# Row numbers by slot: 32 products of 78 columns in place of 64 products of 39

## Chip, core and metric

One core of a Trainium2 chip runs the whole kernel. The metric is the device time of one execution in microseconds (us), from three executions: 375.12, 373.69 and 374.58, median 374.58.

## What is computed

Two layers. The first is a mixture of experts over 2048 tokens of 256 channels: layer norm, a norm over time, a style from a small network, then a router that picks 2 of 8 experts for each token, and the experts (256 to 1024 to 256) on the picked tokens. The second is a finite-difference stencil on the result.

```python
h = h_norm * gamma[:, None, :] + beta[:, None, :]
h_flat = h.reshape(-1, D)
probs = jax.nn.softmax(h_flat @ router_w, axis=-1)
gates, idx = jax.lax.top_k(probs, TOPK)
gates = gates / gates.sum(-1, keepdims=True)
combine = jnp.zeros((N, E), h_flat.dtype).at[jnp.arange(N)[:, None], idx].add(gates)
hid = jax.nn.relu(jnp.einsum('nd,edf->nef', h_flat, exp_w1) + exp_b1)
eout = jnp.einsum('nef,efd->ned', hid, exp_w2) + exp_b2
y = jnp.einsum('ned,ne->nd', eout, combine)
return x + y.reshape(x.shape)
...
df = -gradv_Af + gradvv_Bf * 0.5
f_new = f + df * dt[:, None, None]
return jnp.maximum(f_new, 0.0)
```

## The kernel before

The kernel computes each expert only for the tokens that picked it. The 4096 pairs of token and choice are sorted by expert into columns of 128 rows. There are NC = 39 columns, served in NS = 23 slots; a slot is two columns wide, every third slot is one column wide (`width`).

The prologue norms and transposes the tokens, writes them as rows to DRAM (`h_rows`), and gets the router's logits on the way. VectorE then picks the two experts of each token (lines 1073 to 1091), TensorE counts ranks with products of ones (lines 838 to 844), and VectorE works out the place of each pair: `slot_i`, split into a column number (`col_f`) and a row in the column (`low_f`).

The step that matters here turns places around: for each place it needs the number of the pair that goes there. The pairs lie in TC = TOPK * NJ = 32 tiles of 128. For each tile t, `oh_row[:, :, t]` is a one-hot matrix of pair against row, and `oh_col[:, :, t]` one of pair against column. The number of a pair is 1 + partition + 128 t, in two parts so that each is exact in bf16: `tok[:, 0, :, :]` is `oh_col` times (partition + 1), written by ScalarE (line 551), `tok[:, 1, :, :]` is `oh_col` times 128 t, written by VectorE (line 1154). TensorE multiplies `oh_row` of tile t with each part of `tok` of tile t and sums all 64 products in one psum row of 39 columns (lines 849 to 855). `oh_row` comes in four chunks of eight tiles (lines 1156 to 1161), and TensorE waits for each chunk (`ohrow_ok`). The layout has the tile as the innermost index of `tok`, `oh_row` and `oh_col`.

Behind the last product (`perm_mm`) VectorE reads the psum row: `num_i` is the number as an integer, `src_cur` the source rows of the first two slots, `src_i` those of all, `dst_i` the destinations, with a large number where a place is empty (lines 1162 to 1173). In VectorE's code `link` makes the next instruction wait for this one by a semaphore, and `chained` only counts it, so that the next `link` waits for both.

GpSimd's queue waits for `src_cur` (`src_ok`) and gathers the rows of slots 0 and 1 by indirect DMA (line 735). When the first gather has landed (`rows_in[0]`), three engines go on: TensorE transposes the rows (line 866), VectorE makes the low part of the first expert matrix (line 1184), and SyncE issues the loads of the second expert matrices of slots 0 and 1 (lines 427 to 431). ScalarE and VectorE split every expert matrix into a high and a low part (`w_split`), as they do with the rows and the hidden layer, and TensorE multiplies three pairs of parts. Its order is written out by hand: `turn(0)`, `layer1(0)` with `turn(1)` in its middle, then for each slot k `layer1(k + 1)`, `turn(k + 2)`, `layer2(k)`. ScalarE's order for slot 0 is the split of the second matrix (`split_w2`) ahead of the hidden layer. Results go to DRAM (`y_rows`) by indirect DMA, and the stencil is worked out after the last slot.

Of the kernel before, what the change touches and what calls it, by code (L numbers as in the profile page):

```python
# [7 lines left out]
ALU = mybir.AluOpType  # L8
ACT = mybir.ActivationFunctionType
F32 = mybir.dt.float32  # L10
F32R = mybir.dt.float32r
BF16 = mybir.dt.bfloat16
# [3 lines left out]
P = 128  # L16
NB, T, D = 8, 256, 256
N = NB * T
NJ = N // P
KD = D // P  # L20
E, FF, TOPK = 8, 1024, 2
# [5 lines left out]
NC = ROWS + E - 1  # L27
# [3 lines left out]
EMPTY = 8192.0  # L31
# [89 lines left out]
def moe_then_stencil(nc, x, ids, dt, exp_w1, exp_b1, exp_w2, exp_b2, a_grid, b_grid, small, consts, out):  # L121
# [4 lines left out]
    with ctx:  # L126
        def sb(name, shape, dt_=F32):
            return ctx.enter_context(nc.sbuf_tensor(name, shape, dt_))
# [5 lines left out]
        banks = [psum[:, i, :] for i in range(8)]  # L134
# [7 lines left out]
        dst_i = sb("dst_i", [P, NC], I32)  # L142
# [13 lines left out]
        with ExitStack() as phase:  # L156
            def own(name, shape, dt_=F32):
                return phase.enter_context(nc.sbuf_tensor(name, shape, dt_))
# [15 lines left out]
        with ExitStack() as phase:  # L174
            def own(name, shape, dt_=F32):
                return phase.enter_context(nc.sbuf_tensor(name, shape, dt_))

            h_pre = own("h_pre", [P, KD, N])
            hT = own("hT", [P, KD, N])
            own("w_split_first", [P, 10240])  # L180

            z = own("z", [P, 4, D])
            tok = own("tok", [P, 2, NC, TOPK * NJ], BF16)
            own("w_split_last", [P, 6144 - 1024 - TOPK * NJ * NC])
            h_tok = own("h_tok", [P, NJ, KD, P + E])
            oh_row = own("oh_row", [P, P, TOPK * NJ], BF16)
            oh_col = own("oh_col", [P, NC, TOPK * NJ], BF16)
            eye_rw = own("eye_rw", [P, KD, P + E])
            before_bf = own("before_bf", [P, P], BF16)
            ones_bf = own("ones_bf", [P, P], BF16)  # L190
            st1 = own("st1", [P, NJ, 6])
            mv1 = own("mv1", [P, NJ, 2])
            var1 = own("var1", [P, NJ])
            rs1 = own("rs1", [P, NJ])
            st2 = own("st2", [P, NB, KD, 6])
            mv2 = own("mv2", [P, NB, KD, 2])
            var2 = own("var2", [P, NB, KD])
            rs2 = own("rs2", [P, NB, KD])
            half = own("half", [P, 8])
            warm = own("warm", [P, 8])  # L200
            aff_a = own("aff_a", [P, NB, KD])
            aff_m = own("aff_m", [P, NB, KD])
            aff_b = own("aff_b", [P, NB, KD])

            id_i = own("id_i", [S_SUB, NB], I32)
            id_f = own("id_f", [S_SUB, NB])
            oh_s = own("oh_s", [S_SUB, NB])
            small_sb = own("small_sb", [P, SMALL_ALL])
            se_t = own("se_t", [SE, NB])
            hy1 = own("hy1", [SH, NB])  # L210
            hy2 = own("hy2", [SH, NB])
            sy1 = own("sy1", [SH // 2, NB])
            sty = own("sty", [P, 4, NB])
            gabs = own("gabs", [P, KD, NB])
            grelu = own("grelu", [P, KD, NB])
            gexp = own("gexp", [P, KD, NB])
            gln = own("gln", [P, KD, NB])
            gsum = own("gsum", [P, KD, NB])
            gam = own("gam", [P, KD, NB])

            lg = own("lg", [P, NJ, E])
            eq = own("eq", [P, NJ, E])
            cand = own("cand", [P, NJ, E])
            least = own("least", [P, NJ])
            oh = own("oh", [P, TOPK, NJ, E])
            lg2 = own("lg2", [P, NJ, E])
            gap = own("gap", [P, NJ])
            e2 = own("e2", [P, NJ])
            den = own("den", [P, NJ])
            m_bf = own("m_bf", [P, NJ, E], BF16)  # L230
            cnt_i = own("cnt_i", [P, E], I32)
            tl_i = own("tl_i", [P, 2, E], I32)
            tl_f = own("tl_f", [P, 2, E])
            t_end = own("t_end", [P, 2, E])
            t_off = own("t_off", [P, 2, E])
            base = own("base", [P, E])
            room = own("room", [P, E])
            jump = own("jump", [P, E])
            late = own("late", [P, NJ, E])
            pos = own("pos", [P, NJ, E])  # L240
            pick = own("pick", [P, TOPK, NJ, E])
            slot_f = own("slot_f", [P, TOPK * NJ])
            slot_i = own("slot_i", [P, TOPK * NJ], I32)
            low_i = own("low_i", [P, TOPK * NJ], I32)
            col_i = own("col_i", [P, TOPK * NJ], I32)
            low_f = own("low_f", [P, TOPK * NJ], BF16)
            col_f = own("col_f", [P, TOPK * NJ], BF16)
            row_of = own("row_of", [P, P, TOPK * NJ], BF16)
            col_of = own("col_of", [P, NC, TOPK * NJ], BF16)
            tile_of = own("tile_of", [P, TOPK * NJ], BF16)  # L250
            e_cmp = own("e_cmp", [1, 2, NS, E])
            e_sum = own("e_sum", [1, NS])
            num_i = own("num_i", [P, NC], I32)
            num_f = own("num_f", [P, NC])

        def part(name):
            rows, cols, at = SMALL[name]
            return small_sb[0:rows, at:at + cols]
# [88 lines left out]
        def field(g):  # L347
            return FV[0] if g == 0 else x_sb[:, 4 * g:4 * g + 4, :].rearrange("p j d -> p (j d)")
# [124 lines left out]
        def _(act):  # L473
# [52 lines left out]
            for i in range(NB + 4):  # L526
# [16 lines left out]
                if 0 <= i - 4 < LATE:  # L543
# [4 lines left out]
            act.activation(e2[:, :], gap[:, :], ACT.Exp).then_inc(e2_ok, 1)  # L548

            act.wait_ge(ohcol_ok, 1)  # L550
            act.activation(tok[:, 0, :, :], oh_col[:, :, :], ACT.Copy,
                           scale=cst[:, C_PART + 1:C_PART + 2]).then_inc(tok0_ok, 1)

            def split_w1(k, m, first=False):
# [117 lines left out]
            for g in range(NPAIR):  # L672
# [3 lines left out]
                for i in range(2):  # L676
# [4 lines left out]
                    else:  # L681
                        act.wait_ge(y2_added[g], 16)
                    last = act.activation(FD[g % 2][:, 512 * i:512 * i + 512], field(g)[:, 512 * i:512 * i + 512],
                                          ACT.Copy, scale=dt_b[:, 2 * g + i:2 * g + i + 1])
# [92 lines left out]
        def _(pe):  # L777
# [64 lines left out]
            for j in range(NJ):  # L842
                last = pe.matmul(banks[3][:, 0:E], ones_bf[:, :], m_bf[:, j, :], start=(j == 0), stop=(j == NJ - 1))
# [5 lines left out]
            for t in range(TOPK * NJ):  # L849
                if t % CHUNK == 0:  # L850
                    pe.wait_ge(ohrow_ok, t // CHUNK + 1)
                for part in range(2):
                    last = pe.matmul(banks[1][:, 128:128 + NC], oh_row[:, :, t], tok[:, part, :, t],  # L853
                                     start=(t == 0 and part == 0), stop=(t == TOPK * NJ - 1 and part == 1))
            last.then_inc(perm_mm, 1)

            def turn(k, m):
# [96 lines left out]
            for g in range(NPAIR + 1):  # L954
                if g >= 1:
                    pe.wait_ge(t_s, g)
                    for q in range(2):
                        last = rows_mm(g - 1, q, ident, SM[(g - 1) % 2], q, stop=True)
# [13 lines left out]
        def _(dve):  # L972
            steps = [0]

            def link(ins):

                steps[0] += 1
                ins.then_inc(chain, 1)
                dve.wait_ge(chain, steps[0])

            def chained(ins):

                steps[0] += 1
                ins.then_inc(chain, 1)
# [94 lines left out]
            for c, src in enumerate((lg, lg2)):  # L1079
# [4 lines left out]
                                              op0=ALU.mult, op1=ALU.add))  # L1084
                link(dve.tensor_reduce(least[:, :], cand[:, :, :], AX_X, ALU.min))
                link(dve.tensor_tensor(oh[:, c, :, :], cand[:, :, :], spread(least[:, :]), ALU.is_equal))
                if c == 0:
                    link(dve.scalar_tensor_tensor(out=lg2[:, :, :], in0=oh[:, 0, :, :], scalar=-3e38,
                                                  in1=lg[:, :, :], op0=ALU.mult, op1=ALU.add))
# [32 lines left out]
            def by_token(v):  # L1122
# [6 lines left out]
                                             op0=ALU.mult, op1=ALU.add))  # L1129
# [17 lines left out]
            def by_tile(v, n):  # L1147
                return v.rearrange("p (a t) -> p a t", a=1).broadcast_to([P, n, TC])
# [2 lines left out]
            dve.tensor_tensor(oh_col[:, :, :], by_tile(col_f[:, :], NC), col_of[:, :, :],  # L1151
                              ALU.is_equal).then_inc(ohcol_ok, 1)
            dve.wait_ge(ohcol_ok, 1)
            dve.tensor_tensor(tok[:, 1, :, :], oh_col[:, :, :], by_tile(tile_of[:, :], NC),
                              ALU.mult).then_inc(tok_ok, 1)
            for n in range(TC // CHUNK):
                at = slice(CHUNK * n, CHUNK * n + CHUNK)
# [2 lines left out]
                    low_f[:, at].rearrange("p (a t) -> p a t", a=1).broadcast_to([P, P, CHUNK]), row_of[:, :, at],  # L1160
                    ALU.is_equal).then_inc(ohrow_ok, 1)
            dve.wait_ge(perm_mm, 1)
            num = banks[1][:, 128:128 + NC]

            link(dve.tensor_scalar(num_i[:, :], num, float(N - 1), None, ALU.add))
            dve.tensor_scalar(src_cur[:, :, :], num_i[:, 0:2 * TB].rearrange("p (s t) -> p s t", t=TB), N - 1, None,
                              ALU.bitwise_and).then_inc(src_ok, 2)
            dve.tensor_scalar(src_i[:, 0:NC], num_i[:, :], N - 1, None, ALU.bitwise_and)
            dve.memset(src_i[:, NC:NC + TB], 0)

            link(dve.tensor_scalar(num_f[:, :], num, 0.0, EMPTY, ALU.is_equal, ALU.mult))
            link(dve.scalar_tensor_tensor(out=dst_i[:, :], in0=num, scalar=-1.0, in1=num_f[:, :],
                                          op0=ALU.add, op1=ALU.add))

            def source(k, m):
# [110 lines left out]
            for at, cols in ((slice(0, 4), slice(0, 4)), (slice(4, 8), slice(D - 4, D))):  # L1286
                for n, gi, dst in ((0, 3, edge_w[:, 0, 0:KD, at]), (1, 1, edge_t[:, :, at]),
                                   (2, 4, edge_w[:, 1, 0:KD, at])):
                    last = dve.tensor_tensor(dst, grid[:, gi, :, cols], ew[:, n:n + 1, at].broadcast_to([P, KD, 4]),
                                             ALU.mult)  # L1290
# [114 lines left out]
```

## Time and profile before

| | us |
|---|---|
| median of three executions | 374.58 |
| profiled execution, device time | 374.76 |
| its span from first to last instruction | 373.1 |
| TensorE busy | 315.6 |
| VectorE busy | 288.1 |
| ScalarE busy | 255.1 |
| GpSimd busy | 141.4 |

The span is that of the profiled execution; 1.7 us lie around it. Busy times of different engines lie beside each other, so they do not add up to the span. Durations and starts below are from this one execution.

### The profile page before, as it was taken

The numbers are of one execution on the slowest core, as the hardware profiler recorded it, in microseconds if no ns is written. First come the engines' busy times: TensorE is split into PE (matmuls) and PEld (weight loads), VectorE is DVE, ScalarE is ACT, GpSimd is POOL, SyncE is SP. The second block draws the span as 40 slices with busy tenths as digits, with TensorE's granted clock in tenths as the row PEclk, the third lists the DMA queues.
The fourth block names the chain that finished last, engine by engine and source line by source line (L and its number), as shares of the span: only waits on it lengthen the run. The fifth ranks groups of instructions, "written<-read, shape, count | busy, mean of one in ns | idle before, by whom it ended". The sixth has DMA issues, their size and how long they took to land.

```text
span 373.1 us, 7203 instructions
## 1 busy us (share of the span) xinstructions
PE 315.6 (85%) x2312; PEld 284.2 (76%) x2312; DVE 288.1 (77%) x523; ACT 255.1 (68%) x467; POOL 141.4 (38%) x108
## 2 busy tenths in 40 slices
PE   1684414799999999999999999999999993399996
PEld 1573314799999999999999999999999992143332
DVE  4697791688878878978887886887887771899993
ACT  2577214398799889789789879978978831568211
POOL 1234503122545655553553555565355122101000
PEclk9999755599999999999999999999999999599999
DMA  8902333994777875875875777776575102987411
GB/s 279 352 29 84 114 122 133 283 335 152 263 265 255 285 267 189 280 242 185 278 241 213 258 276 267 245 265 240 181 255 153 43 9 86 302 200 169 113 56 56
DMA packets 49924, 74.83 MB, mean 201 GB/s; under 512 B 3309, under 2 KB 40559, under 8 KB 49776
## 3 DMA queue, kind: packets, MB, share of 16 engines
q1 hardware_dynamic: 45056, 62.13, 49.1%
q0 software_dynamic: 4512, 12.07, 10.9%
q10 hardware_dynamic: 336, 0.39, 0.3%
q8 instruction: 10, 0.16, 0.2%
q14 instruction: 10, 0.08, 0.1%
HBM read 63.56 MB, written 9.31 MB: 195 GB/s over the span
## 4 chain that ended last, share of the span: by engine, by line
PE 74%; DVE 12%; DMA 5%; ACT 3%; POOL 2%; issue 2%; SPq 0%; DVEq 0%; POOLq 0%; ACTq 0%
PE psum L919 30%; PE psum L897 23%; PE psum L945 8%; PE psum L890 5%; PE psum L866 2%; PE psum L892 2%; DMA raw_b<-in_L_cond_exp_w_dram 2%; DMA t_y<-y_rows 1%; PE psum L853 1%; POOL rs L722 1%; DVE st L1014 1%; DMA x_sb<-in_x_dram 1%; POOL rs L718 1%; DMA gathered<-h_rows,src_cur 1%; DVE t_b0f L1361 1%
## 5 line engine op out<-in xcount | busy, mean ns | idle before, releaser
L735 POOL DMA_INDIRECT gathered<-h_rows,src_cur x40 | 76.5, 1912 | 123.8 <-DVE src_cur L1179 75.9
L919 PE MATMUL psum<-w_split,hid 128*128 128x256 f32 x936 | 117.8, 285 | 0.2 <-issue 0.2
L919 PEld LDWEIGHTS psum<-w_split,hid 128*128 128x128 f32 x936 | 113.7, 192 | 0.3 <-issue 0.3
L897 PE MATMUL psum<-slot_h,w_split 128*128 128x256 f32 x768 | 97.2, 287 | 2.4 <-DVE slot_h L1196 2.4
L897 PEld LDWEIGHTS psum<-slot_h,w_split 128*128 128x128 f32 x768 | 95.4, 196 | 3.0 <-issue 3.0
L1190 DVE TENSOR_TENSOR w_split<-raw_b,w_split 128x2048 fp32r<-128x2048 f32 x23 | 52.7, 2292 | 22.6 <-ACT w_split L566 22.6
L589 ACT ACTIVATE relu<-psum,b_cur 128x256 f32<-128x256 f32 x128 | 53.3, 484 | 13.3 <-PE psum L897 11.0
L1184 DVE TENSOR_TENSOR w_split<-raw_a,w_split 128x2048 fp32r<-128x2048 f32 x23 | 52.5, 2282 | 8.0 <-DMA gathered<-h_rows,src_cur 7.0
L598 ACT ACTIVATE hid<-relu 128x512 fp32r<-128x512 f32 (+1 forms) x92 | 50.7, 586 | 9.6 <-DVE relu L1202 9.6
L748 POOL DMA_INDIRECT y_rows<-y_sb,dst_cur x39 | 43.2, 1107 | 27.1 <-issue 11.4
L1213 DVE TENSOR_TENSOR hid<-relu,hid 128x512 fp32r<-128x512 f32 x64 | 42.0, 686 | 10.1 <-ACT hid L598 9.4
L566 ACT ACTIVATE w_split<-raw_b 128x2048 fp32r<-128x2048 f32 x23 | 44.5, 1936 | 4.1 <-DMA raw_b<-in_L_cond_exp_w_dram 4.1
L559 ACT ACTIVATE w_split<-raw_a 128x2048 fp32r<-128x2048 f32 x23 | 44.6, 1939 | 2.9 <-DMA raw_a<-in_L_cond_exp_w_dram 2.9
L890 PE MATMUL psum<-slot_h,w_split 128*128 128x256 f32 x112 | 26.3, 332 | 0.0
L892 PE MATMUL psum<-slot_h,w_split 128*128 128x128 f32 x112 | 24.9, 223 | 0.0
L586 ACT ACTIVATE relu<-psum,b_cur 128x128 f32<-128x128 f32 x56 | 17.4, 363 | 7.8 <-PE psum L892 7.4
L892 PEld LDWEIGHTS psum<-slot_h,w_split 128*128 128x128 f32 x112 | 21.5, 192 | 0.0
L890 PEld LDWEIGHTS psum<-slot_h,w_split 128*128 128x128 f32 x112 | 21.1, 189 | 0.0
L945 PE MATMUL psum<-t_kept,cst 128*128 128x512 f32 x16 | 9.2, 702 | 13.0 <-DVE t_kept L1350 13.0
L1196 DVE TENSOR_TENSOR slot_h<-psum,slot_h 128x512 fp32r<-128x512 f32 (+1 forms) x23 | 14.0, 609 | 5.8 <-ACT slot_h L573 5.3
L866 PE MATMUL psum<-cst,gathered 128*128 128x128 f32 x80 | 13.2, 282 | 5.8 <-DMA gathered<-h_rows,src_cur 5.8
L818 PE MATMUL psum<-eye_rw,hT 128*128 128x136 f32 x64 | 11.5, 331 | 6.9 <-ACT hT L514 6.7
(167 smaller groups left out, 347.8 us busy)
## 6 DMA issues: line engine op xcount, KB each, us to landing
raw_a<-in_L_cond_exp_w_dram SPq DMA_DIRECT2D x23, 1024.0 KB, 5.7
raw_b<-in_L_cond_exp_w_dram SPq DMA_DIRECT2D x23, 1024.0 KB, 5.6
t_y<-y_rows SPq DMA_DIRECT2D x6, 512.0 KB, 9.4
x_sb<-t_y POOLq DMA_DIRECT2D x5, 512.0 KB, 5.0
x_sb<-in_x_dram SPq DMA_DIRECT2D x4, 512.0 KB, 6.8
h_rows<-h_tok SPq DMA_DIRECT2D x16, 128.0 KB, 2.2
out_dram<-t_out SPq DMA_DIRECT2D x3, 512.0 KB, 2.9
b_all<-in_L_cond_exp_b_dram SPq DMA_DIRECT2D x1, 1024.0 KB, 9.7
```

Of the source, the lines that this page charges most:

```text
L559: act.activation(w_split[:, 0, par, 0, :], w1_raw[par], ACT.Copy).then_inc(w1_hi, 1)
L566: act.activation(w_split[:, 1, par, 0, :], w2_raw[par], ACT.Copy).then_inc(w2_hi, 1)
L589: last = act.activation(relu[:, bank, i, :], banks[bank][:, ST * i:ST * i + ST], ACT.Relu, bias=bias)
L598: act.activation(hid[:, par, 0, 2 * bank:2 * bank + 2, 0:n], relu[:, bank, :, 0:n], ACT.Relu if width(k) == 1 else ACT.Copy).then_inc(hid_ ...
L735: pool.indirect_dma_start(out=gathered[:, par, t, :], out_offset=None, in_=h_rows, in_offset=bass.IndirectOffsetOnAxis(ap=src_cur[:, par, ...
L748: pool.indirect_dma_start(out=y_rows, out_offset=bass.IndirectOffsetOnAxis(ap=dst_cur[:, par, t:t + 1], axis=0), in_=y_sb[:, par, t, :], i ...
L890: pe.matmul(both, w_split[:, 0, par, 0, at:at + P], slot_h[:, par, :, k, 0:P], start=(k == 0), stop=False)
L892: last = pe.matmul(both[:, 0, :], w_split[:, 0, par, 1, at:at + P], slot_h[:, par, 0, k, 0:P], start=False, stop=(k == KD - 1))
L897: last = pe.matmul(banks[bank][:, ST * (blk % 2):ST * (blk % 2) + rows], w_split[:, 0, par, w, at:at + P], slot_h[:, par, h, k, 0:rows], s ...
L919: last = pe.matmul(banks[bank][:, D * t:D * t + D], hid[:, par, h, blk, P * t:P * t + P], w_split[:, 1, par, w, D * blk:D * blk + D], star ...
L1184: dve.tensor_tensor(w_split[:, 0, par, 1, :], w1_raw[par], w_split[:, 0, par, 0, :].bitcast(F32), ALU.subtract).then_inc(w1_lo, 1)
L1190: dve.tensor_tensor(w_split[:, 1, par, 1, :], w2_raw[par], w_split[:, 1, par, 0, :].bitcast(F32), ALU.subtract).then_inc(w2_lo, 1)
```

## The change

`tok` is laid out by tile, part and column, so the two parts of one tile are 78 neighbouring columns. TensorE makes one product per tile, with both parts as one moving operand and a psum row of two halves of 39 columns. The two writers of `tok` (ScalarE line 551, VectorE line 1154) keep their reading order and now write with a step of 78 elements. VectorE adds the two halves behind the products: it copies the first half to `num_f`, adds the second and N - 1 into `num_i`, and puts the plain sum into `num_f`; the marks of empty places get a tile of their own, `num_e`.

```diff
-            tok = own("tok", [P, 2, NC, TOPK * NJ], BF16)
+            tok = own("tok", [P, TOPK * NJ, 2, NC], BF16)
...
+            num_e = own("num_e", [P, NC])
...
-            act.activation(tok[:, 0, :, :], oh_col[:, :, :], ACT.Copy,
+            act.activation(tok[:, :, 0, :].rearrange("p t c -> p c t"), oh_col[:, :, :], ACT.Copy,
                            scale=cst[:, C_PART + 1:C_PART + 2]).then_inc(tok0_ok, 1)
...
-                for part in range(2):
-                    last = pe.matmul(banks[1][:, 128:128 + NC], oh_row[:, :, t], tok[:, part, :, t],
-                                     start=(t == 0 and part == 0), stop=(t == TOPK * NJ - 1 and part == 1))
+                last = pe.matmul(banks[1][:, 128:128 + 2 * NC].rearrange("p (h c) -> p h c", h=2), oh_row[:, :, t],
+                                 tok[:, t, :, :], start=(t == 0), stop=(t == TOPK * NJ - 1))
             last.then_inc(perm_mm, 1)
...
-            dve.tensor_tensor(tok[:, 1, :, :], oh_col[:, :, :], by_tile(tile_of[:, :], NC),
+            dve.tensor_tensor(tok[:, :, 1, :].rearrange("p t c -> p c t"), oh_col[:, :, :], by_tile(tile_of[:, :], NC),
                               ALU.mult).then_inc(tok_ok, 1)
...
-            num = banks[1][:, 128:128 + NC]
-
-            link(dve.tensor_scalar(num_i[:, :], num, float(N - 1), None, ALU.add))
+            low, num = banks[1][:, 128:128 + NC], banks[1][:, 128 + NC:128 + 2 * NC]
+
+            link(dve.tensor_copy(num_f[:, :], low))
+            chained(dve.scalar_tensor_tensor(out=num_i[:, :], in0=num, scalar=float(N - 1), in1=num_f[:, :],
+                                             op0=ALU.add, op1=ALU.add))
+            link(dve.tensor_tensor(num_f[:, :], num, num_f[:, :], ALU.add))
...
-            link(dve.tensor_scalar(num_f[:, :], num, 0.0, EMPTY, ALU.is_equal, ALU.mult))
-            link(dve.scalar_tensor_tensor(out=dst_i[:, :], in0=num, scalar=-1.0, in1=num_f[:, :],
+            link(dve.tensor_scalar(num_e[:, :], num_f[:, :], 0.0, EMPTY, ALU.is_equal, ALU.mult))
+            link(dve.scalar_tensor_tensor(out=dst_i[:, :], in0=num_f[:, :], scalar=-1.0, in1=num_e[:, :],
                                           op0=ALU.add, op1=ALU.add))
```

## Rows read from the trace of the kernel before

**Rows 1.** The page: span, busy times, and the granted clock in 40 slices.

```profile
span 373.1 us, 7203 instructions
...
PE 315.6 (85%) x2312; PEld 284.2 (76%) x2312; DVE 288.1 (77%) x523; ACT 255.1 (68%) x467; POOL 141.4 (38%) x108
...
PEclk9999755599999999999999999999999999599999
```

**Rows 2.** The chain of waits from 50 to 100 us: start, length, work.

```profile
54.53 5.45 PE psum L853 x64
...
62.93 2.79 DMA gathered<-h_rows,src_cur
...
65.73 6.37 DMA raw_b<-in_L_cond_exp_w_dram
...
72.12 1.92 ACT w_split L566
...
77.81 5.98 PE psum L897 x48
```

**Rows 3.** The timeline around line 853: start, length, engine, line, operation, count.

```profile
52.98 0.81 DVE L1154 TENSOR_TENSOR tok<-oh_col,tile_of 128x1248 bf16<-128x1248 bf16 x1
52.98 1.33 ACT L551 ACTIVATE tok<-oh_col,cst 128x1248 bf16<-128x1248 bf16 x1 [7.84 <-DVE oh_col L1151]
53.71 2.49 DVE L1158 TENSOR_TENSOR oh_row<-low_f,row_of 128x1024 bf16<-128x1024 bf16 x4
...
54.53 5.43 PE L853 MATMUL psum<-tok,oh_row 128*128 128x39 bf16 x64 [8.14 <-DVE oh_row L1158]
...
56.57 1.97 ACT L559 ACTIVATE w_split<-raw_a 128x2048 fp32r<-128x2048 f32 x1 [2.25 <-DMA raw_a<-in_L_cond_exp_w_dram]
...
60.01 0.20 DVE L1165 TENSOR_SCALAR num_i<-psum 128x39 int32<-128x39 f32 x1 [3.81 <-PE psum L853]
60.31 0.17 DVE L1166 TENSOR_SCALAR src_cur<-num_i 128x4 int32<-128x4 int32 x1
60.39 0.17 DVE L1168 TENSOR_SCALAR src_i<-num_i 128x39 int32<-128x39 int32 x1
60.49 0.19 DVE L1171 TENSOR_SCALAR num_f<-psum 128x39 f32<-128x39 f32 x1
...
60.71 0.20 DVE L1172 SCALAR_TENSOR_TENSOR dst_i<-psum,num_f 128x39 int32<-128x39 f32 x1
```

**Rows 4.** The source view of line 853: shortest, median, longest in ns, first and last start.

```profile
L853 PEld LDWEIGHTS psum<-tok,oh_row x64: 137/152/160, 54.5 to 59.6; 128*128 128x128 bf16 x64
L853 PE MATMUL psum<-tok,oh_row x64: 236/268/282, 54.5 to 59.7; 128*128 128x39 bf16 x64
```

**Rows 5.** Lines 840 and 843: timeline of TensorE, and weight loads by source.

```profile
44.94 1.02 PE L840 MATMUL psum<-m_bf,ones_bf 128*128 128x120 bf16 x15
45.82 0.57 PE L843 MATMUL psum<-m_bf,ones_bf 128*128 128x8 bf16 x16
...
L843 PEld LDWEIGHTS psum<-m_bf,ones_bf x16: 104/104/104, 45.8 to 46.2; 128*128 128x128 bf16 x16
```

**Rows 6.** VectorE's f32 products: a group of the page, and the timeline at 335.72.

```profile
L1190 DVE TENSOR_TENSOR w_split<-raw_b,w_split 128x2048 fp32r<-128x2048 f32 x23 | 52.7, 2292 | 22.6 <-ACT w_split L566 22.6
...
335.72 1.23 DVE L1356 TENSOR_TENSOR t_b2f<-gr,t_fd 128x1024 f32<-128x1024 f32 x1
```

**Rows 7.** Half a microsecond by windows: length, busy times by engine, granted clock, DMA.

```profile
73.50:74.00 0.50, 0.50 (x6) 0.50 (x6) 0.00 (x0) 0.50 (x2) 0.07 (x1) 0.93 1.11 379
```

**Rows 8.** The timeline from 65 us: transposes, VectorE's next work, layer 1 of slot 0.

```profile
65.76 1.12 PE L866 MATMUL psum<-cst,gathered 128*128 128x128 f32 x4 [5.79 <-DMA gathered<-h_rows,src_cur]
65.79 2.29 DVE L1184 TENSOR_TENSOR w_split<-raw_a,w_split 128x2048 fp32r<-128x2048 f32 x1 [4.88 <-DMA gathered<-h_rows,src_cur]
...
68.83 5.19 PE L897 MATMUL psum<-slot_h,w_split 128*128 128x256 f32 x24 [1.96 <-DVE slot_h L1196]
...
74.22 3.11 PE L897 MATMUL psum<-slot_h,w_split 128*128 128x256 f32 x24
```

## The prediction

> **What bounds the kernel now.** First the page. TensorE is busy for 85% of a span of 373.1 us, and in the slices of the granted clock it stands at half speed (1.2 GHz) in a stretch before the expert loop [rows 1]. So most of the time is one engine's, but the change touches only a short prologue step. What that step is worth depends on whether it is on the path, and that is read from the chain of waits. There the 64 products of line 853 stand with 5.45 us, directly behind VectorE's one-hot rows. Behind them come VectorE's row numbers, GpSimd's gather with 2.79 us to its landing, the load of the second expert matrix (6.37 us), its split, and then layer 1 of slot 1 at 77.81 [rows 2]. SyncE issues that load only when the first gather has landed (`sp.wait_ge(rows_in[0], ...)`, line 427), so the gather's time shifts everything behind it. From 77.81 on the chain is nearly all TensorE, up to the tail. A microsecond taken from the products of line 853 is therefore a microsecond of the kernel, unless something else is late.
>
> The timeline of this step gives the schedule: tok's second half on VectorE at 52.98, tok's first half on ScalarE 52.98 to 54.31, four one-hot chunks on VectorE from 53.71, the first product at 54.53, VectorE again at 60.01 [rows 3]. The source view puts the first starts of the 64 products at 54.5 and the last at 59.7, so with 54.53 for the first [rows 3] it is 5.17 us for 63 steps: 82 ns each [rows 4]. All of it ran at the half clock.
>
> **Term 1, the products.** 64 of 39 columns become 32 of 78; the columns streamed stay 2496, while the weight loads halve. What is a product of 78 columns worth? 39 columns at 1.2 GHz are 32 ns, so streaming doesn't set the 82 ns. Two causes are possible. The weights `oh_row[:, :, t]` are read at a step of 32 elements (64 bytes), and so are the moving columns `tok[:, part, :, t]`. The change makes the moving columns contiguous and leaves the weights as they are. The nearest rows are the products of lines 840 and 843, in the same type and at the same clock, with both operands contiguous [rows 5]. The fifteen of line 840 (960 columns, each with its own weight load) take 0.88 us from first start to the first of line 843; 960 columns are 0.80 us. So their loads are hidden behind the stream. The sixteen of line 843, 8 columns each, step by (0.57 - 0.17)/15 = 27 ns, so a contiguous load needs 27 ns at most. One such load lasts 104 ns in the trace; a strided one of line 853 lasts 152 ns [rows 4, 5]. The 48 ns more, on top of 27, make 75 ns, close to the 82. I take from this that the strided weight load sets the pace and stays: 82 ns, with the 65 ns of 78 columns hidden under it. Lower bound: the strided moving read was the cause, 65 + 3 = 68 ns. Upper bound for loads that hide: 82 ns; if load and stream add up, 82 - 32 + 65 = 115 ns (a rival, below).
>
> The Trainium skill has a rule that points to the lower bound: "TensorE: Matmul & The Clock Gate" (section "Weight-path perf modes") says that the fast load of 128 weights of a type other than fp32 reads them packed or strided, with steps up to 1,024 elements. If a strided load is really as fast as a packed one, the strided moving columns must be what takes 82 ns, and the sum goes by 68 ns: the first rival below. The longer loads in the trace (152 against 104 ns) speak against it.
>
> **Term 2, tok's second half on VectorE (line 1154).** It now writes with a step of 78 elements instead of contiguously. At present it takes 0.81 us for 1248 elements of bf16 [rows 3]. A full-rate f32 product takes 2292 ns for 2048 elements and about 1.23 us for 1024, so 1.04 ns for each element and 0.17 us fixed [rows 6]. By that rate 1248 elements take 1.46 to 1.47 us, which shows that line 1154 now runs at nearly twice it. I take it that the step loses this double rate: +0.65 us. Bounds: 0 (the rate is kept; the one-hot chunks write runs of 8 elements at a 64-byte step and still take 0.68 us for 1024), and +1.3 us if every write cost double. VectorE has nothing else there, so the four one-hot chunks start later by as much. TensorE waits for the first chunk, so its first start goes from 54.53 to 55.18.
>
> The Trainium skill speaks against the change here: "VectorE: DVE Perf Modes" (section "Mode 2x_1P") wants 16-bit elements at a step of +1 or -1 for two results a cycle. No row before has a fully strided 16-bit write, so no run here shows it yet; by the rule the sum has the +0.65 us, without it the sum is 0.65 us lower.
>
> **Term 3, tok's first half on ScalarE (line 551).** Same strided write; 1.33 us for 1248 elements [rows 3], which is already one element per 1.07 ns. I cost it at nothing: it ends at 54.31, and the first one-hot chunk, which ended at 53.71 + 0.68 = 54.39, now ends near 55.04. That cover is 0.7 us; a ScalarE write slower than 2.0 us would show. ScalarE's next work, the split of raw_a, starts at 56.57, when its load has landed [rows 3], and is not touched.
>
> **Are the chunks in time?** The fourth chunk ends at 53.71 + 2.49 = 56.20 before, 56.85 after [rows 3]; the 25th product would start by its own pace at 55.18 + 24 x 0.082 = 57.15. Yes at 82 ns, no at 68 ns: then the last eight start at about 56.99 (the 0.14 us from chunk to product kept), and the faster pace is worth only part of itself.
>
> **Term 4, VectorE behind the products (lines 1162 to 1176).** One instruction on the psum row and one link become: copy the first half, link, add with N-1 into num_i, and num_f on its heels, link. From num_i to src_cur is now 0.30 us; a linked pair of this size steps by 0.22 us (lines 1171 to 1172), an unlinked one by about 0.1 (lines 1166 to 1168) [rows 3]. So +0.22 for the copy and +0.10 for num_f: +0.32 us, up to +0.45 if the step behind the psum copy is 0.30 as well. All of it is on the path to src_cur and the gather. What comes behind src_cur (src_i, num_e, dst_i) is hidden by VectorE's idle time up to 65.79 [rows 8].
>
> **Sum.** The last product starts at 55.18 + 31 x 0.082 = 57.72 instead of 59.70: -1.98. Its 39 more columns: +0.03. Term 4: +0.32. Together -1.63 us at src_cur, and a rigid shift of all that follows. Against the profiled execution (374.76 us, of which 373.1 us are span and 1.7 us lie around it) this is 373.1 us. The median of 374.58 is 0.2 us lower, so by it 372.9; I say 373.1.
>
> **What could be late next.** Layer 1 of slot 0 starts at 68.83 at the half clock, its first 24 products take 5.19 us (216 ns each), and the other 24 start at 74.22, after the clock rose between 73.5 and 74.0 [rows 7, 8]. At full clock 48 products take 5.98 us, 125 ns each [rows 2]. Shifted by 1.6 us the first half starts at 67.2 and ends at 72.4; the four transposes of slot 1, which took 1.12 us for slot 0 at half clock [rows 8], follow, partly in that time, to about 73.2. If the clock rose at the same absolute time, the second half would end at about 76.4, and layer 1 of slot 1 wants to start at 76.2. So the slack there is used up, and this costs 0 to 0.2 us: inside the range.
>
> **Rivals.**
> - *Full gain at the products or in tok.* With a pace of 68 ns the chunks limit: last start 56.99 + 7 x 0.068 = 57.47, sum -1.88 us, 372.9. If line 1154 keeps its double rate: -2.3 us, 372.5. For: runs of 8 elements keep it. Against: here no two neighbours are adjacent.
> - *Load and stream add up* (115 ns): last start 58.74, sum -0.6 us, 374.2. For: 82 is 50 + 32. Against: line 840, where they don't add.
> - *The clock stays low longer.* After a shorter burst at 1.2 GHz the clock comes back later than 73.5. Each microsecond of delay costs 1 - 125/216 = 0.42 us on layer 1 of slot 0. With a rise at 77.1 the gain is gone; with all of it at half clock the second half ends at 73.2 + 5.2 = 78.4, 0.6 us later than slot 1 starts now: 375.4. For: the 5.4 us burst of line 853 didn't lift the clock. Against: it rose after TensorE had been busy for 4.7 us from 68.83, and that burst is not shortened.
> - *Pace by columns, not by products (the slower side).* If the strided reads cost 2.1 ns per column of the product and went on doing so, 78 columns take 165 ns: the last start is 55.18 + 5.12 = 60.30, the sum +0.9 us, 375.7. The change loses from a pace of 135 ns on. Against: the moving columns are contiguous afterwards, and line 840 streams those at 0.9 ns each.
>
> **How the numbers follow.** Forecast (82 ns, down to about 75; double rate lost) 0.5; full gain 0.3; adding up 0.12; cold clock 0.04; by columns 0.04. A measurement of this kernel tells about 0.5% (1.87 us) from no change. The forecast is 0.2 us short of that, and the full-gain case straddles it: faster 0.3. Slower by that much would take more than either slow rival gives, but with the scatter of runs (373.69 to 375.12) I leave 0.04. Same 0.66. The range takes in the full gain with the double rate kept (372.5, less 0.2 for the median) and the adding up with some cold clock: 372.3 to 374.5.
>
> **What would show it.** The 32 products: first start near 55.2, step 82 ns (68 to 75: the moving read was the cause; 115: they add up; 165: by columns). Line 1154 at 1.46 us. Four VectorE instructions between the last product and src_cur, 0.6 to 0.7 us from the first start to src_cur's start. First gather landing near 64.1 instead of 65.73, and layer 1 of slot 1 at 76.2 instead of 77.81. If the gather is earlier and slot 1 isn't, the clock or the load of the second matrix took the gain.

## The result and the profile after

The changed kernel takes 376.49 us (median of six runs, 376.11 to 378.63), against 374.69 us for the kernel before (six runs, 373.69 to 375.12). The ratio is 1.0054 with a 95% interval of 1.0036 to 1.0072: it is slower, by 1.8 us or 0.5%. The profiled execution took 376.34 us with a span of 374.7 us. The forecast was 373.1 us, with a range of 372.3 to 374.5 us.

The page after, for the busy times in [rows 1] (PE is TensorE, PEld its weight loads, DVE VectorE, ACT ScalarE, POOL GpSimd):

```profile
span 374.7 us, 7141 instructions
...
PE 313.7 (84%) x2280; PEld 282.5 (75%) x2280; DVE 293.2 (78%) x525; ACT 258.9 (69%) x467; POOL 142.5 (38%) x108
```

TensorE is 1.9 us less busy; the products of line 853 alone take 3.0 us less (2.44 against 5.43). VectorE is 5.1 us busier and ScalarE 3.8. The timeline of the changed kernel, which answers to [rows 3], shows where (start, length, engine, line):

```profile
52.45 0.81 DVE L1151 TENSOR_TENSOR oh_col<-col_f,col_of 128x1248 bf16<-128x1248 bf16 x1
53.30 5.49 DVE L1154 TENSOR_TENSOR tok<-oh_col,tile_of 128x1248 bf16<-128x1248 bf16 x1
53.30 5.60 ACT L552 ACTIVATE tok<-oh_col,cst 128x1248 bf16<-128x1248 bf16 x1 [7.85 <-DVE oh_col L1151]
...
58.42 2.66 DVE L1158 TENSOR_TENSOR oh_row<-low_f,row_of 128x1024 bf16<-128x1024 bf16 x4
59.42 2.31 PEld L853 LDWEIGHTS psum<-tok,oh_row 128*128 128x128 bf16 x32 [12.81 <-ACT tok L552]
59.45 2.44 PE L853 MATMUL psum<-tok,oh_row 128*128 128x78 bf16 x32 [12.75 <-DVE oh_row L1158]
61.92 0.20 DVE L1165 COPY num_f<-psum 128x39 f32<-128x39 f32 x1 [0.84 <-PE psum L853]
62.15 0.20 DVE L1166 SCALAR_TENSOR_TENSOR num_i<-psum,num_f 128x39 int32<-128x39 f32 x1
62.27 0.19 DVE L1168 TENSOR_TENSOR num_f<-psum,num_f 128x39 f32<-128x39 f32 x1
62.56 0.17 DVE L1169 TENSOR_SCALAR src_cur<-num_i 128x4 int32<-128x4 int32 x1
```

The two writes of tok take 5.49 and 5.60 us in place of 0.81 and 1.33. The products and the adding behind them went as the change wants. And the chain of waits, for [rows 2], now runs through the VectorE write:

```profile
53.30 5.49 DVE tok L1154
...
59.45 2.45 PE psum L853 x32
...
65.18 2.79 DMA gathered<-h_rows,src_cur
67.99 6.45 DMA raw_b<-in_L_cond_exp_w_dram
74.46 1.92 ACT w_split L567
...
80.16 5.98 PE psum L897 x48
```

**The account.** Where oh_col starts differs from trace to trace by up to 1.4 us (52.13 before, 52.45 after, 53.53 in e3), so I measure the step from the start of oh_col to the start of src_cur. In the trace of before oh_col stands just ahead of [rows 3]:

```profile
52.13 0.81 DVE L1151 TENSOR_TENSOR oh_col<-col_f,col_of 128x1248 bf16<-128x1248 bf16 x1
```

The step is 60.31 - 52.13 = 8.18 us before and 62.56 - 52.45 = 10.11 us after: +1.93. It is made of +4.60 up to the first product (7.00 against 2.40), -3.00 from there to the first VectorE instruction behind the products (2.47 against 5.48, rounded), and +0.34 for the adding (0.64 against 0.30). Layer 1 of slot 1 starts at 80.16 instead of 77.81, later by the 0.32 us of the start, the 1.93 us of the step and 0.1 us of the weight load. The products of the experts end at 312.99 instead of 310.65, still 2.34 us later. In the tail behind them 0.7 us came back in these two profiled executions, most of it in the first load of results (4.88 us in the chain of after, 5.52 us in that of before). No run tests that part.

### The profile page after: what moved, and what is told of

Its sections match the earlier page's. It is cut to its first block, busy times and chain, and to the rows that moved or that the text cites. A ratio compares the mean times of both kernels' runs of the same rounds, so it can differ in the third digit from the quotient of the medians.

```text
span 374.7 us, 7141 instructions
## 1 busy us (share of the span) xinstructions
PE 313.7 (84%) x2280; PEld 282.5 (75%) x2280; DVE 293.2 (78%) x525; ACT 258.9 (69%) x467; POOL 142.5 (38%) x108
## 4 chain that ended last, share of the span: by engine, by line
PE 74%; DVE 12%; DMA 5%; ACT 3%; issue 2%; POOL 2%; SPq 0%; DVEq 0%; POOLq 0%; ACTq 0%
PE psum L919 30%; PE psum L897 23%; PE psum L945 8%; PE psum L890 5%; PE psum L866 2%; PE psum L892 2%; DMA raw_b<-in_L_cond_exp_w_dram 2%; DVE tok L1154 1%; DMA t_y<-y_rows 1%; PE psum L819 1%; DMA x_sb<-in_x_dram 1%; POOL rs L719 1%; ACT h_pre L507 1%; DMA gathered<-h_rows,src_cur 1%; DVE st L1014 1%
## 5 line engine op out<-in xcount | busy, mean ns | idle before, releaser
L749 POOL DMA_INDIRECT y_rows<-y_sb,dst_cur x39 | 44.4, 1138 | 25.9 <-issue 11.4
L819 PE MATMUL psum<-eye_rw,hT 128*128 128x136 f32 x64 | 12.3, 356 | 6.4 <-ACT hT L515 6.4
```

Source lines behind the costliest of these rows:

```text
L749: pool.indirect_dma_start(out=y_rows, out_offset=bass.IndirectOffsetOnAxis(ap=dst_cur[:, par, t:t + 1], axis=0), in_=y_sb[:, par, t, :], i ...
```

## The experiments

The edits of e1 to e4 are shown against the changed kernel, that of e5 against the kernel before, and those of e6 and e8 against the experiment ahead of each. Ratios are to the kernel before on the same chip (medians 374.96 us beside e1 to e4, 375.23 us beside the others).

**e1: the two writes one after the other.**

```diff
             dve.wait_ge(ohcol_ok, 1)
+            dve.wait_ge(tok0_ok, 1)
             dve.tensor_tensor(tok[:, :, 1, :].rearrange("p t c -> p c t"), ...
```

> The changed kernel, but VectorE waits for ScalarE's half of tok (tok0_ok) before it writes its own, so that the two strided writes don't overlap. In the changed kernel they overlapped and took 5485 ns (VectorE) and 5604 ns (ScalarE) for 1248 elements, 4.4 ns each. Theory A, a strided 16-bit write costs this by itself on either engine: about 5.6 us for ScalarE and then 5.5 us for VectorE, first product 5.6 us later than in the changed kernel, time about 382 us. Theory B, the two engines hold each other up because they write at the same time: 1.34 us for ScalarE and 1.46 us for VectorE, first product about 2.7 us earlier than in the changed kernel, about 373.5 us. A half-way case (shared path, each write costs half as much alone): 2.7 and 2.7 us, and the time unchanged at 376.3 us.

Measured: 381.98 us in one run, as theory A has it. Its timeline:

```profile
53.59 5.55 ACT L552 ACTIVATE tok<-oh_col,cst 128x1248 bf16<-128x1248 bf16 x1 [7.86 <-DVE oh_col L1151]
...
59.24 5.49 DVE L1155 TENSOR_TENSOR tok<-oh_col,tile_of 128x1248 bf16<-128x1248 bf16 x1 [5.68 <-ACT tok L552]
```

Each engine takes alone what it takes beside the other. Theory B and the half-way case fall. The price belongs to the access pattern, and it is the same on both engines.

**e2: the step on the reading side.**

```diff
-            act.activation(tok[:, :, 0, :].rearrange("p t c -> p c t"), oh_col[:, :, :], ACT.Copy,
+            act.activation(tok[:, :, 0, :], oh_col[:, :, :].rearrange("p c t -> p t c"), ACT.Copy,
...
-            dve.tensor_tensor(tok[:, :, 1, :].rearrange("p t c -> p c t"), oh_col[:, :, :], by_tile(tile_of[:, :], NC),
+            dve.tensor_tensor(tok[:, :, 1, :], oh_col[:, :, :].rearrange("p c t -> p t c"),
+                              tile_of[:, :].rearrange("p (t a) -> p t a", a=1).broadcast_to([P, TC, NC]),
```

> The changed kernel, but both engines take oh_col in the order of tok: they read at a step of 32 elements (64 bytes) and write runs of 39 neighbouring elements. If only strided writes are dear: VectorE 1.46 us (or less), ScalarE 1.34 us, first product near 55.2, time 372.9 us or 1.5 to 2 us below the kernel before. If a strided 16-bit access is as dear for reads as for writes: about 5.5 us each again and 376.3 us.

Measured: 372.55 us, ratio 0.9936 (0.9913 to 0.9959) to the kernel before. The same transposition now costs:

```profile
53.10 2.32 DVE L1154 TENSOR_TENSOR tok<-oh_col,tile_of 128x1248 bf16<-128x1248 bf16 x1
53.10 2.46 ACT L552 ACTIVATE tok<-oh_col,cst 128x1248 bf16<-128x1248 bf16 x1 [7.86 <-DVE oh_col L1151]
```

Neither expectation holds: a strided 16-bit read isn't free (1.46 us was expected for VectorE and 1.34 for ScalarE), but it costs less than half of the strided write. With that alone the change is faster than the kernel before. From oh_col to src_cur it is 7.04 us (59.30 - 52.26) against 8.18, 1.14 less. The ratio of the times says more (1.5 to 3.3 us). In the profiled executions (372.61 against 374.76 us) 1.3 us of the gain are there when the experts' products end (309.35 against 310.65). The other 0.8 us lie in the tail behind them, where the first load of results takes 4.48 us against 5.52; no run tests that part.

**e3: one wide product on the old layout.**

```diff
-            tok = own("tok", [P, TOPK * NJ, 2, NC], BF16)
+            tok = own("tok", [P, 2, NC, TOPK * NJ], BF16)
...
-                                 tok[:, t, :, :], start=(t == 0), stop=(t == TOPK * NJ - 1))
+                                 tok[:, :, :, t], start=(t == 0), stop=(t == TOPK * NJ - 1))
```

Both writers go back to contiguous writes; the adding stays.

> The kernel before with its layout of tok and its contiguous writes, but one product per tile whose moving operand is 78 columns at a step of 64 bytes, and the halves added by VectorE as in the changed kernel. If the strided moving read sets the pace (82 ns for 39 columns, 2.1 ns each): 165 ns a product, 32 of them as long as the 64 before, plus 0.34 us for the adding: 0.3 to 0.5 us slower than the kernel before, 375.1 us. If the weight load had set it: 82 ns a product, 2.2 us faster, 372.4 us.

Measured: 374.79 us, ratio 0.999 (0.9966 to 1.0014): no change. In its source view of line 853 the products start from 55.9 to 60.5:

```profile
L853 PE MATMUL psum<-tok,oh_row x32: 310/328/337, 55.9 to 60.5; 128*128 128x78 bf16 x32
```

That is (60.46 - 55.93)/31 = 146 ns for 78 strided columns, 1.9 ns a column, where 165 ns were expected. So the strided moving columns, not the number of products, set most of the pace of the kernel before. From 82 to 146 ns the 39 more columns cost 1.6 ns each, which leaves 18 ns a product of before; what these are isn't shown, since no run has strided moving columns with contiguous weights. A pace by columns, as in the last rival, is real as long as the columns are strided. The fewer products win 0.6 us and the adding takes back 0.3.

**e4 and e4b: the new layout without a strided write.** oh_col and the tables of column and tile numbers are laid out by tile and column as well, with one empty column as padding.

```diff
-            tok = own("tok", [P, TOPK * NJ, 2, NC], BF16)
+            tok = own("tok", [P, TOPK * NJ, 2, NC + 1], BF16)
-            oh_col = own("oh_col", [P, NC, TOPK * NJ], BF16)
+            oh_col = own("oh_col", [P, TOPK * NJ, NC + 1], BF16)
...
-            dve.tensor_tensor(tok[:, :, 1, :].rearrange("p t c -> p c t"), oh_col[:, :, :], by_tile(tile_of[:, :], NC),
+            dve.tensor_tensor(tok[:, :, 1, :], oh_col[:, :, :], tile_of[:, :, :],
```

> The new layout of tok without any strided write: oh_col and the numbers of columns and tiles are laid out by tile and column as well, with 40 columns in place of 39 (the last one is empty), so every operand of the three writers is contiguous but for the one that repeats col_f over the columns. Expected: oh_col 0.8 to 1.5 us, tok's halves 0.83 us (VectorE) and 1.37 us (ScalarE), first product at 54.6 to 55.3, 32 products of 80 columns at 67 ns held back by the one-hot chunks, last one near 57.2: 1.5 to 2.3 us faster than the kernel before, about 372.7 us. If the layout as such were dear (whatever writes it), it would be as slow as the changed kernel, 376.4 us.

> The kernel of e4 again, beside e6 on the same chip: 1.6 to 1.9 us faster than the kernel before; from the start of oh_col to the start of src_cur 6.24 us as in e4, since the scatter of about 1 us comes from ahead of oh_col.

Measured: 373.19 us, ratio 0.9957 (0.9935 to 0.9978), and as e4b, on another chip, 371.99 us, ratio 0.9919 (0.9901 to 0.9938). This version is faster than both kernels. Timeline of e4b:

```profile
52.74 1.49 DVE L1151 TENSOR_TENSOR oh_col<-col_f,col_of 128x1280 bf16<-128x1280 bf16 x1
54.27 0.82 DVE L1154 TENSOR_TENSOR tok<-oh_col,tile_of 128x1280 bf16<-128x1280 bf16 x1
54.27 1.36 ACT L552 ACTIVATE tok<-oh_col,cst 128x1280 bf16<-128x1280 bf16 x1 [8.54 <-DVE oh_col L1151]
55.01 2.49 DVE L1158 TENSOR_TENSOR oh_row<-low_f,row_of 128x1024 bf16<-128x1024 bf16 x4
55.81 2.33 PEld L853 LDWEIGHTS psum<-tok,oh_row 128*128 128x128 bf16 x32 [8.91 <-ACT tok L552]
55.84 2.47 PE L853 MATMUL psum<-tok,oh_row 128*128 128x80 bf16 x32 [8.85 <-DVE oh_row L1158]
```

From oh_col to src_cur it is 6.24 us in both (58.98 - 52.74 in e4b), 1.94 less than before, as expected. The layout isn't dear; the way it was written is. The time of e4 (1.8 us below the kernel before) fits its expectation, that of e4b doesn't: 1.6 to 1.9 us were expected, and the medians differ by 3.2 us (2.3 to 3.7 by the interval). The step explains 1.94 of them. The two profiled executions differ by 2.0 us (372.77 against 374.76), so the rest isn't in the traces. The intervals of the two ratios hardly overlap. The oh_col of e4 starts at 53.46 and that of e4b at 52.74; what moves it isn't settled.

**e5: the write by itself.** On the kernel before, behind dst_i, one instruction of 512 elements at a time.

```diff
+            for n, (o, i) in enumerate(cases()):
+                act.activation(o, i, ACT.Copy).then_inc(probe_act, 1)
...
+            for o, i in cases():
+                link(dve.tensor_tensor(o, i, i, ALU.mult))
+            dve.sem_inc(probe_dve, 1)
+            dve.wait_ge(probe_act, len(cases()))
```

> The kernel before with instructions added behind the row numbers, each alone and linked by a semaphore, first on VectorE, then on ScalarE: 512 elements written at a step of 1, 2, 4, 8, 16 and 78 bf16 elements, in runs of 1, 2, 4 and 8 neighbours at a step of 78, in f32 at a step of 1, 2 and 39, and last the reading side at a step of 78 (bf16) and 39 (f32). Two theories of the 4.4 ns of a strided write. Theory W, only writes smaller than 4 bytes are dear (a 2-byte write that can't be paired has to read and put back its word): step 2 to 78 all cost 4.4 ns, f32 at any step 1.0 ns, runs of 2 at step 78 about 1 ns. Theory L, a write is dear where it goes to another line than the last one: bf16 cheap at steps of 1 to 4, dear from a step of 8 or 16 on; f32 at step 39 as dear as bf16 at 78; runs of 2 half, of 4 a quarter of the price per element. The added work makes this kernel some 15 us slower; only the durations are asked for.

Measured on VectorE, in the order of the expectation: nine bf16 writes (step 1, 2, 4, 8, 16, 78, then runs of 2, 4 and 8 at step 78), three f32 writes (step 1, 2, 39), the bf16 read at step 78 and the f32 read at step 39:

```profile
63.58 0.47 DVE L1210 TENSOR_TENSOR probe_b<-probe_s 128x512 bf16<-128x512 bf16 x1
64.09 0.73 DVE L1210 TENSOR_TENSOR probe_b<-probe_s 128x512 bf16<-128x512 bf16 x1
64.85 1.36 DVE L1210 TENSOR_TENSOR probe_b<-probe_s 128x512 bf16<-128x512 bf16 x1
66.25 2.44 DVE L1210 TENSOR_TENSOR probe_b<-probe_s 128x512 bf16<-128x512 bf16 x1
68.72 2.29 DVE L1210 TENSOR_TENSOR probe_b<-probe_s 128x512 bf16<-128x512 bf16 x1
71.05 2.32 DVE L1210 TENSOR_TENSOR probe_b<-probe_s 128x512 bf16<-128x512 bf16 x1
73.40 0.63 DVE L1210 TENSOR_TENSOR probe_b<-probe_s 128x512 bf16<-128x512 bf16 x1
74.07 0.46 DVE L1210 TENSOR_TENSOR probe_b<-probe_s 128x512 bf16<-128x512 bf16 x1
74.56 0.43 DVE L1210 TENSOR_TENSOR probe_b<-probe_s 128x512 bf16<-128x512 bf16 x1
75.02 0.69 DVE L1210 TENSOR_TENSOR probe_b<-probe_s 128x512 f32<-128x512 f32 x1
75.75 0.69 DVE L1210 TENSOR_TENSOR probe_b<-probe_s 128x512 f32<-128x512 f32 x1
76.48 1.09 DVE L1210 TENSOR_TENSOR probe_b<-probe_s 128x512 f32<-128x512 f32 x1
77.60 1.09 DVE L1210 TENSOR_TENSOR probe_s<-probe_b 128x512 bf16<-128x512 bf16 x1
78.73 1.09 DVE L1210 TENSOR_TENSOR probe_s<-probe_b 128x512 f32<-128x512 f32 x1
```

ScalarE gives nearly the same where a step is dear: 2.46 us at step 8, 2.36 at 78, 0.67 for runs of 2, 1.13 for f32 at step 39 and for the two reads 1.13 and 1.14, against 0.63 contiguous. The run took 404.16 us, 29 us more than the kernel before, where some 15 were expected; only its durations are used.

Neither theory is the whole. Less 0.17 us fixed [rows 6], VectorE pays for each lone 2-byte write 1.1 ns at step 2, 2.3 at 4, 4.4 at 8, and no more beyond (4.1 at 16, 4.2 at 78). For each 16 bytes touched the first three are 4.4, 4.6 and 4.4 ns. The 1.1 ns at step 2 are also just the full rate of [rows 6], so that row alone shows no price of the step. Where 4 bytes are written together, a jump costs 1.8 ns (f32 at step 39; runs of two bf16 at step 78: 0.46 us for 256 jumps), and a strided read costs 1.8 ns as well. So there are two prices: 1.8 ns for an access elsewhere, 4.1 to 4.4 ns if it writes only 2 bytes there. That a 2-byte write must read and put back what is around it would explain the second price; it is argued, not shown.

The Trainium skill's note on cachelines ("SBUF — State Buffer", section "Door 1: The DMA port swizzle") says that SBUF has 16-byte lines and that each access crossing to a new one pays. The 4.4 ns for each 16 bytes, with no rise beyond a step of 16 bytes, agrees with it. The note also lets bf16 elements stride within such a line for free, and there the measurement decides otherwise for lone writes: 2.3 ns at a step of 4 elements, two to a line, against 0.6 ns contiguous. It has no number, and it doesn't tell a 2-byte write from a read.

**e6 and e8: which operand paces the products.** e6 is e4 with 64 products of 40 contiguous columns again, and e8 is e6 with the one-hot rows laid out by tile, so that the weights are contiguous too.

```diff
-                last = pe.matmul(banks[1][:, 128:128 + 2 * (NC + 1)].rearrange("p (h c) -> p h c", h=2), oh_row[:, :, t],
-                                 tok[:, t, :, :], start=(t == 0), stop=(t == TOPK * NJ - 1))
+                for part in range(2):
+                    last = pe.matmul(banks[1][:, 128:128 + NC + 1], oh_row[:, :, t], tok[:, t, part, :],
+                                     start=(t == 0 and part == 0), stop=(t == TOPK * NJ - 1 and part == 1))
```

And for e8, with the writing and the reading of oh_row turned accordingly:

```diff
-            oh_row = own("oh_row", [P, P, TOPK * NJ], BF16)
+            oh_row = own("oh_row", [P, TOPK * NJ, P], BF16)
```

> The layout without strided writes (e4), but 64 products again, one per part, of 40 contiguous columns each, all in one psum row, so that VectorE has nothing to add up. The weights are still read at a 64-byte step. If the strided moving columns alone set the 82 ns of before: 34 ns a product, 64 as long as the 32 of e4, and 0.34 us less on VectorE: 0.3 us faster than e4, some 2.2 us faster than before. If the strided weight load has a floor of its own near 66 ns (hidden so far under 78 columns): 66 ns a product, last start 1.6 us later than in e4, and about 1.3 us slower than e4.

> The 64 products of 40 contiguous columns (e6), with the one-hot rows laid out by tile as well, so that the weights are read contiguously too. If the strided weight load is the floor of 62 ns that e6 showed: 34 ns a product (40 columns at 1.2 GHz) within a chunk. If 62 ns is the floor of any such product at the half clock: 62 ns again. The one-hot chunks repeat low_f over the columns and so should fall to the full rate of oh_col in e4, 1.2 us each instead of 0.68, so TensorE waits for chunks: eight tiles of it take 0.55 us and the chunk 1.1 us, and the kernel is no faster than e4, about 373.5 to 374.5 us.

Measured for e6: 374.68 us, ratio 0.9986 (0.9971 to 1.0002), beside e4b with 371.99. First start 56.52, last 60.45: 62 ns a product, near the second case of its expectation. From oh_col to src_cur it is 7.60 us, 1.36 more than in e4b; the medians differ by 2.7 us, so here too e4b is faster than its step explains. For e8: 375.17 us in one run, 0.7 us above what was expected, and 33 to 34 ns a product within a chunk (the sixteen of a chunk take 0.69 to 0.72 us, of which 0.20 are the last one's own length). The source views of e6 (loads and products) and of e8 (loads):

```profile
L854 PEld LDWEIGHTS psum<-tok,oh_row x64: 138/163/183, 56.5 to 60.4; 128*128 128x128 bf16 x64
L854 PE MATMUL psum<-tok,oh_row x64: 221/228/237, 56.5 to 60.5; 128*128 128x40 bf16 x64
```

```profile
L854 PEld LDWEIGHTS psum<-tok,oh_row x64: 104/112/118, 56.9 to 60.7; 128*128 128x128 bf16 x64
```

So the strided weight load has a floor of 62 ns, which a product of 78 contiguous columns (65 ns of streaming) just hides, and a contiguous one is hidden under 34 ns. e8 gains nothing from it, because its one-hot chunks take 4.62 us for four instead of 2.49, as its timeline shows:

```profile
55.53 4.62 DVE L1159 TENSOR_TENSOR oh_row<-low_f,row_of 128x1024 bf16<-128x1024 bf16 x4
...
57.94 0.72 PE L854 MATMUL psum<-tok,oh_row 128*128 128x40 bf16 x16 [0.35 <-DVE oh_row L1159]
```

The fast-load rule of the Trainium skill ("TensorE: Matmul & The Clock Gate", section "Weight-path perf modes") reads weights packed or strided. Strided they do load, but here at 62 ns and not under 34, so it is no promise of equal speed.

## Why the prediction was wrong, step by step

- **Term 2 failed, the strided write on VectorE.** The row gave 0.81 us, I added 0.65 for the lost double rate and held +1.3 for the worst. It was +4.68 us (5.49). The upper bound was no bound: "every write cost double" had no row behind it. The nearest strided rows (one-hot chunks in runs of 8 elements) fill 16 bytes at a time and so show nothing of the price; e5 gives 4.1 to 4.4 ns for a lone 2-byte write at a step of 8 elements or more (5.49 us is 4.3 ns, less the same 0.17 us) against 0.6 ns for a contiguous one.
- **Term 3 failed the same way.** ScalarE's write, costed at nothing under a cover of 0.7 us, took 5.60 us (+4.3). With VectorE's mended alone, ScalarE's would still have held TensorE back. The prediction named the cover, but not that both engines would miss it together. It also held ScalarE's next work, the split of raw_a, untouched; that started at 58.38 instead of 56.57, and ended long before ScalarE was needed again at 69.17.
- **Term 1: the choice between load and moving read was wrong, to the kernel's good.** I took 82 ns, by the strided weight load. The products step by 66 ns within a chunk, with gaps of 0.13 and 0.12 us where TensorE waits for chunks three and four. e3 shows that the strided moving read set the pace of before (146 ns at 78 columns), e6 that the strided load alone allows 62 ns. The 75 ns that I derived from the durations of the loads (48 ns more on top of 27) overshot by 13. The full-gain rival had the mechanism right: by it the first and the last product start 2.29 us apart (57.47 - 55.18), by my sum 2.54, and measured are 2.17.
- **Term 4 held:** 0.34 us against 0.32.
- **The rigid shift held:** a step 1.93 us longer moved layer 1 of slot 1 by 2.35 us, 0.32 of it from ahead of the step. With terms 2 and 3 replaced by what they measured, and term 1 as well, the sum gives the measured step: 7.00 - 2.40 up to the first product in place of 0.65, that is -1.63 + 3.95 = +2.3, less 0.4 for the faster products: +1.9 us.
- **The rivals.** The slow side was given to other mechanisms ("by columns", the low clock), and neither happened. The clock rose between 76.0 and 76.5 in the kernel after, 5 us behind the start of layer 1 of slot 0 (71.09), against 4.7 us before [rows 7, 8]. That lag isn't constant: it rose between 71.0 and 71.5 in e2 and e4, some 3 us behind their starts (67.87 and 68.27), and between 73.0 and 73.5 in e4b, nearly 6 us behind its own (67.53). All three have the shorter burst of 32 products that the rival feared; what sets the lag isn't settled. The mechanism of the slower side stood in my own text as a bound of term 2, and I cut it off at twice the rate.
- **"The slack there is used up" can be seen in e4b.** Its layer 1 of slot 0 starts at 67.53, 1.30 us earlier than before, but the clock rose only between 73.0 and 73.5, and the chain goes through TensorE in place of the load of the second matrix. It cost nothing: the experts' products end at 309.12, 1.53 us earlier than before. The chain in its view from 50 to 80 us (the last row is cut off at 80):

```profile
67.53 5.46 PE psum L897 x24
72.98 0.64 PE psum L866 x4
73.63 6.48 PE psum L897 x54
```

The Trainium skill's rule for the double rate ("VectorE: DVE Perf Modes", section "Mode 2×_1P") is right that the step loses it: in e5 a step of 2 elements takes 1.1 ns each against 0.6. But the fallback that the same page describes (section "Mode 1× (REGULAR)"), one result a cycle, weird strides included, is not what this write showed: 1.46 us by the full rate of [rows 6], 5.49 us measured.

## What to carry to other kernels

Before a layout is turned to please TensorE, ask who writes it: a bf16 element written alone, 16 bytes or more from the last one, costs VectorE and ScalarE 4.1 to 4.5 ns where a contiguous one costs 0.6 and 1.0. Put the transposition where no element is written alone: into the tables and one-hots that can be generated in the new order (e4), or on the reading side (e2). By the step e4 is the better one (6.24 us against 7.04); the times of the two on the same chip (373.19 and 372.55 us) don't show it. And an upper bound needs a row that has the same pattern down to the bytes written together; where there is none, the range must say so.

## What the runs showed of the hardware

- A lone 2-byte write at a step of 16 bytes or more costs 4.1 to 4.4 ns on VectorE and, less 0.14 us fixed (0.63 us for 512 contiguous elements, 1.33 us for 1248), 4.3 to 4.5 ns on ScalarE, whether the other engine writes or not (5.49 and 5.55 us alone, 5.49 and 5.60 together). Two neighbours written together at a step of 156 bytes cost VectorE 0.9 ns each.
- A strided access of 2 or 4 bytes that isn't a lone 2-byte write costs VectorE 1.8 ns at a step of 156 bytes: bf16 and f32 reads, f32 writes. The bf16 read of e2 at a step of 64 bytes costs 1.7 ns (2.32 us for 1248). An f32 write at a step of 8 bytes costs 1.0 ns, as a contiguous one. TensorE's moving columns cost nearly the same, 146 ns for 78 (1.9 ns each) against 66 ns contiguous at the half clock.
- A strided bf16 weight load paces products at 62 ns at the half clock; a contiguous one is hidden under 34 ns.
- Repeating an operand over the innermost elements takes VectorE's bf16 product from the double to the full rate: 1.49 us for the 1280 elements of oh_col in e4, where the same comparison takes 0.81 us for 1248 elements in the kernel after, with the operand repeated over the outer elements.
